# Leaky maximum ahead of one exponential, two sets of banks for turned weights, VectorE frees slots

## The reference

```python
e = leaky_relu(concat(h[src], h[dst], ef) @ W_attn + b_attn, 0.01)[:, 0]
m = concat(h[src], ef) @ W_ne
emax = segment_max(e, dst); ex = exp(e - emax[dst])
alpha = ex / segment_sum(ex, dst)[dst]
z = segment_sum(alpha[:, None] * m, dst)
out = layernorm(x + relu(concat(x, z) @ W_out))
```

## Time and profile before

| what | value |
|---|---|
| median of 3 runs | 4924.11 us (4914.36 to 4927.84) |
| the profiled execution's own time | 4937.21 us |
| its span | 4935.4 us |
| GpSimd busy | 3304.1 us (67%) |
| VectorE busy | 2651.7 us (54%) |
| ScalarE busy | 2267.7 us (46%) |
| TensorE busy, matmul and weight load | 2110.4 us (43%), 1948.9 us (39%) |
| mean granted TensorE clock | 0.646 |
| DMA | 127 GB/s mean, engines about 45% busy |

### The profile page before, as it was taken

The page is one execution under the profiler, slowest core; times in us unless marked ns, Lnnn a source line. Parts: engine busy times, 40 slices in busy tenths (PEclk is TensorE's granted clock), DMA queues, the critical chain, the costliest instruction groups (busy, mean ns, idle before and its releaser), DMA issues.

```text
span 4935.4 us, 65300 instructions
## 1 busy us (share of the span) xinstructions
PE 2110.4 (43%) x10260; PEld 1948.9 (39%) x10261; DVE 2651.7 (54%) x5260; ACT 2267.7 (46%) x4123; POOL 3304.1 (67%) x3149
## 2 busy tenths in 40 slices
PE   1444444444443444444444444444443444344446
PEld 0444434434433433334334333443333434343436
DVE  5555555555555555555555555555554555555557
ACT  1544445544444444445444444444444444444444
POOL 6566666666767766667666766666666677666751
PEclk8666666666566666566655656666666666666666
DMA  4444444444444444444444444444444444444441
GB/s 112 122 129 128 128 124 136 129 129 133 134 127 124 139 129 127 129 129 139 123 123 139 129 133 125 132 136 126 131 129 118 139 132 137 127 131 129 129 129 54
DMA packets 409572, 628.94 MB, mean 127 GB/s; under 512 B 208412, under 2 KB 208796, under 8 KB 409332
## 3 DMA queue, kind: packets, MB, share of 16 engines
q1 hardware_dynamic: 296164, 519.51, 32.8%
q0 software_dynamic: 100096, 102.60, 11.4%
q10 hardware_dynamic: 13072, 4.80, 0.5%
HBM read 621.58 MB, written 4.81 MB: 127 GB/s over the span
## 4 chain that ended last, share of the span: by engine, by line
issue 29%; DVE 20%; another core or an unknown queue 18%; DVEq 15%; ACT 12%; ACTq 5%; PE 1%; POOL 0%
DVE u L636 5%; DVE e L705 4%; DVE prod L631 4%; DVEq L760 3%; ACT psS L506 2%; ACT pT L468 2%; DVEq L727 2%; DVEq L698 2%; ACTq L520 2%; ACT acc L478 2%; DVE acc L698 2%; ACT zs L515 2%; ACT zb L516 1%; DVE bounds L750 1%
## 5 line engine op out<-in xcount | busy, mean ns | idle before, releaser
L373 POOL DMA_INDIRECT V<-in_x_dram,srcs x3128 | 3278.7, 1048 | 1509.2 <-issue 904.3
L866 PE MATMUL psT<-ident,e 128*128 128x128 f32 x3136 | 829.7, 416 | 2764.5 <-DVE e L705 1528.6
L866 PEld LDWEIGHTS psT<-ident,e 128*128 128x128 f32 x3136 | 597.5, 216 | 2921.0 <-DVE e L705 1601.7
L872 PE MATMUL psG<-V,pT 128*128 x6288 | 1367.0, 389 | 0.0
L872 PEld LDWEIGHTS psG<-V,pT 128*128 128x128 f32 x6288 | 1312.4, 306 | 0.1
L468 ACT COPY pT<-psT 128x512 f32<-128x512 f32 x785 | 451.5, 575 | 1410.0 <-remote 1364.1
L631 DVE TENSOR_TENSOR prod<-V,wa 128x512 f32<-128x512 f32 x782 | 506.8, 690 | 587.2 <-issue 587.1
L705 DVE TENSOR_TENSOR e<-zb,zs 128x1024 f32<-128x1024 f32 x392 | 478.8, 1221 | 268.5 <-remote 191.8
L746 DVE CUSTOM_DVE_ANT_0 um<-ubc,psS 128x1024 f32<-128x1024 f32 x391 | 477.4, 1221 | 157.8 <-issue 88.6
L636 DVE TENSOR_REDUCE u<-prod 128x8 f32<-128x1024 f32 x391 | 477.0, 1220 | 46.2 <-issue 12.1
L698 DVE SCALAR_TENSOR_TENSOR acc<-psG,half,acc x788 | 244.7, 349 | 396.9 <-issue 259.2
(11 more groups left out here) (97 smaller groups left out, 615.9 us busy)
## 6 DMA issues: line engine op xcount, KB each, us to landing
ubc<-scores SPq DMA_DIRECT2D x391, 512.0 KB
dbc<-in_dst_dram SPq DMA_DIRECT2D x390, 512.0 KB
V<-in_edge_attr_dram SPq DMA_DIRECT2D x390, 256.0 KB
V<-in_x_dram,srcs POOLq DMA_INDIRECT x3128
scores<-u SPq DMA_DIRECT2D x391, 4.0 KB
srcs<-in_src_dram SPq DMA_DIRECT2D x390, 4.0 KB
out_dram<-y SPq DMA_DIRECT2D x12, 256.0 KB
xt<-in_x_dram ACTq DMA_DIRECT2D x6, 448.0 KB
```

The lines of the kernel that those rows point to most:

```text
L373: nc.gpsimd.indirect_dma_start(Vx[0:n, s, j, 0:F], None, x[:, :], bass.IndirectOffsetOnAxis(ap=srcs[0:n, s, j:j + 1], axis=0)).then_inc(h_ ...
L866: last = nc.tensor.transpose(psT[:, i, j * P:(j + 1) * P], e1[:, :].rearrange("q (p j) -> q j p", j=J)[:, 4 * i + j, :], ident[:, :])
L872: last = nc.tensor.matmul(psG[:, bass.ds(bk, 1), 0:AW].rearrange("p a f -> p (a f)"), pT[:, i, j * P:(j + 1) * P], V[:, bass.ds(sv + XW * ...
```

## The change

1. **One exponential.** um is completed by VectorE ahead of the exponential. ScalarE writes 0.01 um + 0.01 (score of the node) into psS, over the Square that um has used (the wait low_done), VectorE takes max(um + score of the node, psS) in place in um, reading psS (lr_done), and ScalarE takes one exponential of it straight to e1. The tiles zb and zs, the second exponential and weigh go. node and wnode get two more columns for the node's score and a hundredth of it; ebias becomes dif, one column.
2. **Two sets of banks.** psT gets four banks, two per supertile by its parity (s % 2). psG keeps one bank. TensorE turns both halves of the window's e1 right after the exponential, then waits for VectorE's merge of the next window's place in the order (merged >= G + 1) and multiplies the window before. Sums reach psG one step after their weights are turned.
3. **Order.** ScalarE: nbias, Square, linear pass, dif, alpha, rescale, exponential, both pT halves. VectorE: merge first, then both wnode steps, um, bounds, nn, node, leaky maximum, then prod and score.
4. **Frees.** The psR transpose goes. VectorE waits for agg_done at a supertile's start and increments v_free of the slot of three supertiles ago (BEHIND from 2 to 3).
5. **Node pairs.** TensorE waits for VectorE's prod of the supertile before it takes the pair, VectorE waits for the pair before (y_ready) ahead of its next prod. ScalarE's y_pair keeps its place.

```diff
-BEHIND = 2
+BEHIND = 3
...
-        psT = ps("psT", [P, 2, 512])
-        psG = ps("psG", [P, 2, 512])
-        psR = ps("psR", [P, 512])
+        psT = ps("psT", [P, 4, 512])
+        psG = ps("psG", [P, 512])
...
             def weights_out(G, i):
 
+                turned = act.snap(banks[1], min_val=0, max_val=2)
                 act.wait_ge(tr[i], G)
-                act.wait_ge((agg_half, agg_done)[i], G)
-                nc.scalar.copy(pT[:, i, :], psT[:, i, :]).then_inc(pt[i], 1)
+                act.wait_ge((agg_half, agg_done)[i], G + 1)
+                nc.scalar.copy(pT[:, i, :], psT[:, bass.ds(turned + i, 1), :].rearrange("p a e -> p (a e)")).then_inc(pt[i], 1)
...
                     nc.scalar.activation(psS[:, :], dbc[:, s % 2, :], ACT.Square, bias=nbias[:, 0:1], scale=FAR).then_inc(sq_done, 1)
+                    act.wait_ge(wn1, G)
+                    act.wait_ge(cmax_done, G)
+                    nc.scalar.activation(psS[:, :], um[:, :], ACT.Identity, bias=wnode[:, 4:5], scale=SLOPE).then_inc(low_done, 1)
+                    act.wait_ge(nn_done, G)
+                    nc.scalar.activation(dif[:, :], wnode[:, 2:3], ACT.Identity, bias=nn[:, 0:1], scale=-1.0).then_inc(dif_done, 1)
+                    act.wait_ge(lowf_in, 16)
+                    act.wait_ge(dif_done, G + 1)
+                    nc.scalar.activation(alpha[:, bass.ds(act.snap(slots[0], min_val=0, max_val=LAG), 1), :].rearrange("p a k -> p (a k)"),
+                                         half[:, bass.ds(t, 1), :].rearrange("p a k -> p (a k)"), ACT.Exp, scale=dif[:, 0:1])
+                    rescale(G)
+                    act.wait_ge(tr[0], G)
+                    act.wait_ge(tr[1], G)
+                    act.wait_ge(lr_done, G + 1)
+                    nc.scalar.activation(e1[:, :], um[:, :], ACT.Exp, bias=nn[:, 0:1]).then_inc(e_done, 1)
+                    weights_out(G, 0)
                     weights_out(G, 1)
-                    rescale(G)
...
-                    nc.scalar.activation(zs[:, :], um[:, :], ACT.Exp, bias=ebias[:, 1:2], scale=SLOPE)
-                    nc.scalar.activation(zb[:, :], um[:, :], ACT.Exp, bias=ebias[:, 0:1]).then_inc(e_done, 1)
-                    weights_out(G, 0)
...
+                if left >= 1:
+                    dve.wait_ge(agg_done, dve.snap(g))
+                    dve.sem_inc(v_free[(s - BEHIND) % RING], 1)
...
+                    merge(G)
                     dve.wait_ge(node_set, G)
                     dve.wait_ge(u_in[r], scored)
...
-                    weigh(G)
...
-                    merge(G)
+                    dve.wait_ge(low_done, G)
+                    nc.vector.scalar_tensor_tensor(um[:, :], um[:, :], wnode[:, 3:4], psS[:, :], ALU.add, ALU.max).then_inc(lr_done, 1)
                     pass_on()
...
+                    if y_steps is not None:
+                        dve.wait_ge(y_ready, y_steps + 1)
                     edge_product(s2).then_inc(prod_done, 1)
...
-                    pe.wait_ge(mx_done, G)
-                    pe.wait_ge(pt[0], G)
-                    turn(0)
-                if multiplies:
-                    pe.wait_ge(pt[0], G)
-                    pe.wait_ge(merged, G)
-                    multiply(0, sv, bk)
-                pe.wait_ge(pt[1], G)
-                if turns:
-                    turn(1)
-                if multiplies:
-                    multiply(1, sv, bk)
+                    free = pe.snap(room)
+                    pe.wait_ge(pt[0], free)
+                    pe.wait_ge(pt[1], free)
+                    pe.wait_ge(e_done, G + 1)
+                    turn(0, r)
+                    turn(1, r)
+                pe.wait_ge(merged, G + 1)
+                for i in range(2):
+                    pe.wait_ge(pt[i], G + 1)
+                    multiply(i, sv)
...
-                    nc.tensor.transpose(psR[0:32, 0:P], ident[:, 0:32], ident[:, :]).then_inc(v_free[(s - BEHIND) % RING], 1)
...
                     if s < YS:
+                        pe.wait_ge(prod_done, RING * k + s + 1)
                         y_pair(YS * k + s)
```

More of the change, by code:

```diff
@@ L697, in merge @@
                     row = accv[:, bass.ds(bb + i, 1), :].rearrange("p a f -> p (a f)")
-                    last = nc.vector.scalar_tensor_tensor(row, psG[:, bass.ds(bk, 1), 0:AW].rearrange("p a f -> p (a f)"), half[:, bass.ds(tb, 1), i], row, ALU.mult, ALU.add)
+                    last = nc.vector.scalar_tensor_tensor(row, psG[:, 0:AW], half[:, bass.ds(tb, 1), i], row, ALU.mult, ALU.add)
                 last.then_inc(merged, 1)
-            def weigh(G):
-                dve.wait_ge(e_done, G)
-                dve.wait_ge(tr[1], G)
-                nc.vector.tensor_tensor(e1[:, :], zb[:, :], zs[:, :], ALU.max).then_inc(mx_done, 1)
             def pass_on():
@@ L711, in pass_on, with supertile @@
                     dve.reg_mov(block_of[i], dve.snap(block_of[i - 1]))
-                dve.reg_mov(spare, dve.snap(bank[0]))
-                dve.reg_mov(bank[0], dve.snap(bank[1]))
-                dve.reg_mov(bank[1], dve.snap(spare))
                 dve.reg_add(g, g, 1)
-            def supertile(k, s, left):
+            def supertile(k, s, left, y_steps=None):
                 t = RING * k + s
@@ L768, in supertile @@
                     dve.wait_ge(u_done, t + 3)
-            with dve.Fori(0, TURNS - 1) as k:
+            with dve.Fori(0, YT) as k:
                 for s in range(RING):
-                    supertile(k, s, RING)
+                    supertile(k, s, RING, YS * k + min(s, YS))
+            with dve.Fori(YT, TURNS - 1) as k:
+                for s in range(RING):
+                    supertile(k, s, RING, PAIRS + 1)
             for s in range(RING):
-                supertile(TURNS - 1, s, RING - s)
+                supertile(TURNS - 1, s, RING - s, PAIRS + 1)
             supertile(TURNS, 0, 0)
             for i in range(LAG):
-                if i == 0:
-                    weigh(dve.snap(g))
                 merge(dve.snap(g))
                 pass_on()
-            dve.wait_ge(merged, dve.snap(g))
+            dve.wait_ge(merged, dve.snap(g) - 1)
             step(nc.vector.tensor_scalar(rl[:, :], accv[:, 0:NB, F], TINY, None, ALU.max))
@@ L828, in _ @@
             pe.wait_ge(w_in, 16 * 6)
-            nc.tensor.transpose(psG[0:F, 0, 0:P], wne[:, :], ident[:, :]).then_inc(wt_ready, 1)
+            nc.tensor.transpose(psG[0:F, 0:P], wne[:, :], ident[:, :]).then_inc(wt_ready, 1)
             pe.wait_ge(wt_copied, 1)
-            nc.tensor.matmul(psG[:, 0, P:P + F], wneT[:, :], wo_z[:, :], start=True, stop=True).then_inc(wz_ready, 1)
+            nc.tensor.matmul(psG[:, P:P + F], wneT[:, :], wo_z[:, :], start=True, stop=True).then_inc(wz_ready, 1)
             def y_turn():
@@ L851, in _, with turn, multiply @@
             count = pe.alloc_register("count_pe")
-            slot = [pe.alloc_register(f"slot_{i}_before") for i in range(LAG)]
-            bank = [pe.alloc_register("bank_pe"), pe.alloc_register("other_bank_pe")]
-            spare = pe.alloc_register("bank_spare_pe")
-            pe.reg_mov(bank[0], 1)
-            pe.reg_mov(bank[1], 0)
-            for i in range(LAG):
+            slot = [pe.alloc_register(f"slot_{i}_before") for i in range(2)]
+            for i in range(2):
                 pe.reg_mov(slot[i], 0)
             pe.reg_mov(g, 1)
-            pe.wait_ge(pt_clear, 1)
+            room = pe.alloc_register("room_pe")
             pe.sem_inc(pt[0], 1)
-            def turn(i):
+            pe.sem_inc(pt[1], 1)
+            pe.sem_inc(y_ready, 1)
+            def turn(i, r):
                 for j in range(4):
-                    last = nc.tensor.transpose(psT[:, i, j * P:(j + 1) * P], e1[:, :].rearrange("q (p j) -> q j p", j=J)[:, 4 * i + j, :], ident[:, :])
+                    last = nc.tensor.transpose(psT[:, 2 * r + i, j * P:(j + 1) * P],
+                                               e1[:, :].rearrange("q (p j) -> q j p", j=J)[:, 4 * i + j, :], ident[:, :])
                 last.then_inc(tr[i], 1)
-            def multiply(i, sv, bk):
+            def multiply(i, sv):
                 for j in range(4):
-                    last = nc.tensor.matmul(psG[:, bass.ds(bk, 1), 0:AW].rearrange("p a f -> p (a f)"), pT[:, i, j * P:(j + 1) * P],
+                    last = nc.tensor.matmul(psG[:, 0:AW], pT[:, i, j * P:(j + 1) * P],
                                             V[:, bass.ds(sv + XW * (4 * i + j), 2 * (EF_AT - 4 * i - j))].rearrange("p (k w) -> p k w", k=2)[:, :, 0:XW],
```

99 lines of the change are left out of this document (46 added, 53 removed).

## The result

| | before | after |
|---|---|---|
| median | 4922.14 us (4 runs, 4914.36 to 4927.84) | 5636.27 us (4 runs, 5608.98 to 5651.88) |
| ratio | | 1.1446, 95% interval 1.1395 to 1.1498 |
| profiled execution's own time, span | 4937.21, 4935.4 | 5646.3, 5644.4 |
| mean granted TensorE clock | 0.646 | 0.584 |
| DMA | 127 GB/s | 111 GB/s |

The account below looks back on a forecast made before the run. It took the mean step as a balance: GpSimd's 10.8 us of gathers plus its pauses, with VectorE alone at 8.8. From 4937 us, minus 158 (gathers) plus 77 (node pairs) gave 4856, median 4843; range 4480 to 5170.

Parts of the forecast that it names:

- The maximum from PSUM, gathers shorter: GpSimd: gathers beside the new maximum no longer stretch, 0.51 us per supertile, 158 us saved, bounds 0 to 257.
- the same pauses: GpSimd: its pauses stay as before the change, 1.4 us per supertile, while the gathers get shorter.
- Frees at zero: VectorE's freeing of slots at its next start: taken as zero, between a 434 us gain and a loss from mid-supertile waits.
- (c): Frees come late: GpSimd waits for VectorE's next start, 7.1 us on 103 pauses, +279 us, median 5122; chance 0.17.
- TensorE and ScalarE's order, "ordinary steps pay nothing": New order of turning, multiplying and copies: ScalarE ends 1.2 us before um needs it; a mark 5 us late still costs.
- VectorE's chain, 9.1 us: VectorE's own step grows 0.3 us from 8.80 to 9.1, hidden under GpSimd's 10.3, so costing nothing.
- Node pairs, +77 us (30 to 270): First 70 supertiles: um waits 5.5 us for Square behind the pair's copy, 14.3 us such a step, 77 us lost.
- (b): Node pairs decide, slower: gathers' gain not realised since slow stretches set the step; median 5001 us; chance 0.22.
- (a): GpSimd's pauses go too, once frees move off TensorE: step 10.3 us, median 4424 us; chance 0.15.

Follow-up runs that it names:

- late_pe_frees_again: Changed kernel with ScalarE's weight copies behind the next Square and frees by TensorE two supertiles back, run again: 4886.78 us, ratio 1.0055.
- set 3: Runs where the kernel before took 4329 us; changed kernel with frees by TensorE two supertiles back 0.995, with late copies as well 0.9498.
- set 4: Runs where the kernel before took 4858 us; changed kernel 1.1018, with frees by TensorE two supertiles back 1.0305, with late copies as well 1.0055.
- late copies: ScalarE's copies of the turned weights moved behind the next Square, pair copies a supertile later; alone in the changed kernel 4992.79 us, ratio 1.0297.
- set 1: Runs of single edits, kernel before 4851 us; changed kernel with late copies 4992.79 us, with VectorE's frees ahead of prod two supertiles back 5204.84 us.
- the runs with four gathers: Four of each supertile's eight gathers left out: changed kernel 4057.31 us, kernel before 3810.13 us.
- after_drain8: Changed kernel with GpSimd waiting ahead of each supertile's first gather until the eight before have landed: 5132.54 us, ratio 1.0568.
- after_copies_late: Changed kernel with ScalarE's weight copies moved behind the next Square, node pairs' copies one supertile later, VectorE's frees kept: 4992.79 us, ratio 1.0297.
- late_free_mid: Changed kernel with late copies and VectorE's frees given ahead of prod for the supertile two back: 4939.14 us, ratio 1.0165.

## Why the prediction was wrong, step by step

- **The maximum from PSUM, gathers shorter: the mechanism right, its worth not there.** Gathers went from 1.051 to 0.956 us, 0.76 us per supertile, more than the 0.51 taken and near the bound of 0.83. The guess that a gather waits for the end of the maximum in which it begins is borne out record by record. The passage of the Trainium skill that spoke against it ("SBUF — State Buffer", "Who interferes with whom") infers that such operations don't hold up descriptor generation; this trace disagrees, the maximum with two SBUF inputs did stretch the gathers. But the 158 us assumed "the same pauses". late_pe_frees_again shows that the pauses grow by most of what the gathers give: 1.9 us a supertile for the 1.46 that the rows give (the prediction wrote 1.4), and the step is 12.06 us for 12.16. Only where GpSimd never pauses (set 3) sets the gathers' length the step; how much of the ratio of 0.950 it makes there, no run tells.
- **Frees at zero: the step that failed.** "If GpSimd runs dry in mid-supertile it waits for the next start" stood there as the loss, and rival (c) priced it at 7.1 us a pause, on one supertile in three. The pause measured 7.0 us, but on 164 of 311 supertiles, and the 709 us it adds overran the price of 279. With the frees alone given back to TensorE, and a supertile sooner, 348 of 497 us come back (set 4). The price per pause was right and the number of pauses was not, and that could have been read from the rows: the earlier trace rows have 173 pauses in 310 supertiles, not 103, and 173 x 7.1 = 1228 us is near the 1156 measured. That the pauses did not grow fewer as they grew longer has its reason in the trace: a longer pause goes with a longer slow step, in which ScalarE's register instructions now stand ahead of Square, and after it GpSimd finds two slots free and runs sixteen gathers, into the next slow stretch (154 such runs of sixteen, 122 before).
- **TensorE and ScalarE's order, "ordinary steps pay nothing".** True of steps outside slow stretches: 8.8 us. The slack of "1.2 us before um needs them" was worked out with register instructions at their fast price. In a slow stretch some sixteen slots of 0.70 us stand between the copies and nbias. ScalarE's register work was in no step of the prediction, although VectorE's 2.78 us ahead of its first small instruction showed the same slowness. What the copies' place costs by itself depends on the frees: with VectorE's frees at its start, the step behind the pairs was 12.2 us with late copies (set 1) against 12.9 to 13.7 with early ones (other sets, so not a clean comparison); with TensorE's, nothing (set 4).
- **VectorE's chain, 9.1 us:** 8.8 in a fast step and 8.4 after the last gather; small and hidden, as forecast.
- **Node pairs, +77 us (30 to 270): the mechanism right, undersized.** um waited 6.75 us for 5.5, the step was 17.1 us in the mean for 14.3, and without slow stretches a pair cost 6.3 us (the runs with four gathers). Late copies won back 120 us in set 4 and 194 us in set 3. The mean over ten was taken too kindly: the steps without a pair took 12.7 us for the 11.65 forecast. And its lower bound of 30 us was no bound: at 4.0 us a pair, the forecast's own steps give (7 x 12.8 + 3 x 11.65) / 10 = 12.46 us for 12.42, 2 to 3 us in all.
- **Rivals.** (c) was the right one at 0.17, beside (b)'s pairs; the two were priced as alternatives and came together: +477 and +220 us. (a) needed increments that are prompt; set 3 is that case, and there the change as a whole, whose own run fell into none such, stays unmeasured.

What stays open: why register instructions take 0.70 us and TensorE's increments come late while GpSimd gathers without rest, and why not in set 3, whose gathers run at the same speed. The runs show the tie, not the cause. The two effects also come apart: after_drain8 has hardly a slow record, but late increments. That after_copies_late gains in the long stretch through ScalarE's queue, not through the frees, is argued from its timeline only.

## What to carry to other kernels

Before a free or any other signal is moved to another engine, ask where that engine will stand when the waiting one has run dry, and how often that is; "half a step" costs on every pause, and the pause itself then changes the rhythm. Put no queue's register work, copies or waits ahead of the one instruction that the next engine waits for if there is slack behind it. And compare variants within one set of runs: here the same kernel took 4329 and 4935 us, and which limit ruled changed with it.

## What the runs showed of the hardware

- While GpSimd issued indirect gathers without a pause, register instructions of SyncE, VectorE and ScalarE took 0.70 us instead of 0.05 to 0.1, from about the sixth gather on, and the increments of agg_done by TensorE came 3 to 19 us after the multiply's end (late_pe_frees_again, a quarter and 95% of them are below these); in late_free_mid most of TensorE's increments came 1.5 us or more into GpSimd's next pause. With four gathers a supertile there was no such stretch. Breaks of 0.3 us did not end the stretches, waits for the landing (1.8 us) did, though agg_done stayed 2.4 to 3.6 us late.
- In set 3 none of this showed, for the same instructions, and the kernel before took 4329 us.
- A gather that began while a maximum over two SBUF tiles ran ended about 0.82 us after that maximum's end (298 gathers, 1.53 us in the mean); one that had begun before it was not stretched. A maximum over one SBUF and one PSUM tile stretched none of 190 gathers (0.954 us at most).
